# Unpadded weight tiles: a graph attention kernel whose matmuls load 125 columns instead of 128

## What is computed

```python
q = (x @ Wq + bq).reshape(n, H, C)      # k and v likewise, n = 3125, C = 128
alpha = jnp.einsum('ehc,ehc->eh', q[dst], k[src]) / jnp.sqrt(jnp.float32(C))
p = jnp.exp(alpha - amax[dst])          # amax: the largest alpha of each dst
denom = jax.ops.segment_sum(p, dst, num_segments=n) + 1e-16
out = jax.ops.segment_sum(p[:, :, None] * v[src], dst, num_segments=n)
out = out / denom[:, :, None]
out = out.reshape(n, H * C) if concat else out.mean(axis=1)
return out + x @ Ws + bs
...
h = jax.nn.relu(layer1); out = layer2(h); result = layernorm(x + out)
```

## Time and profile before

| | us |
|---|---|
| median of 3 runs | 2020.97 (2019.72 to 2021.14) |
| the profiled execution, its own time | 2020.97 |
| its span in the profile | 2019.2 |
| PE busy | 1820.1 (90%), 14788 matmuls |
| PEld busy | 1356.7 (67%) |
| DVE busy | 1603.9 (79%) |
| ACT busy | 1241.7 (61%) |
| POOL busy | 1162.1 (58%) |

### The profile page before, as it was taken

One profiled execution on the slowest core, in us unless ns is written; L12 is line 12 of the kernel. 1 busy time (PEld: TensorE's weight loads), 2 busy tenths in 40 slices (PEclk: granted clock), 3 DMA queues, 4 the chain that ended last, 5 costly groups with the idle time before them and its releaser, 6 DMA issues. The chain is left out here.

```text
span 2019.2 us, 44528 instructions
## 1 busy us (share of the span) xinstructions
PE 1820.1 (90%) x14788; PEld 1356.7 (67%) x14788; DVE 1603.9 (79%) x4613; ACT 1241.7 (61%) x2055; POOL 1162.1 (58%) x1481
## 2 busy tenths in 40 slices
PE   2876657999999999999999999949889999999998
PEld 1456654777777777777777777736557777777776
DVE  3799986888888888888888888722478888898886
ACT  2665444776777677777777776722156666766666
POOL 3310004776777677767776767611247777767775
PEclk8877778999999999999999999979989999999999
DMA  5059985887788788877877877670169889899996
GB/s 122 1 132 229 229 218 121 155 159 150 150 150 158 146 154 154 154 148 151 157 152 146 154 154 153 119 219 12 30 140 177 171 175 179 168 181 177 169 181 116
DMA packets 771458, 303.31 MB, mean 150 GB/s; under 512 B 657154, under 2 KB 751086, under 8 KB 767979
## 3 DMA queue, kind: packets, MB, share of 16 engines
q1 hardware_dynamic: 767323, 296.42, 73.4%
q10 hardware_dynamic: 3266, 2.36, 0.5%
q0 software_dynamic: 640, 1.63, 0.3%
HBM read 94.57 MB, written 48.45 MB: 71 GB/s over the span
## 5 line engine op out<-in xcount | busy, mean ns | idle before, releaser
L1335 PE MATMUL score_l<-KT,QT_l 128*128 128x512 f16 (+2 forms) x3150 | 772.9, 355 | 13.4 <-DVE piece_max_l L1188 13.0
L1188 DVE CUSTOM_DVE_ANT_0 prob_l<-score_l,mask_l 125x512 f32<-125x512 f32 (+2 forms) x1050 | 642.6, 614 | 166.1 <-PE score_l L1335 162.0
L1037 POOL TENSOR_TENSOR prob_parts_l<-prob_l,prob_parts_l 125x512 f16<-125x512 f32 x600 | 722.2, 1234 | 16.6 <-ACT prob_parts_l L1116 16.6
L1107 ACT ACTIVATE prob_l<-prob_l,neg_max_l 125x1024 f32<-125x1024 f32 (+1 forms) x450 | 524.6, 1166 | 126.6 <-DVE neg_max_l L1196 126.5
L1366 PE MATMUL output_l<-V,prob_flipped_l 128*128 128x256 f16 x2400 | 459.5, 272 | 1.5 <-DMA prob_flipped_l<-prob_parts_l 1.3
L1368 PE MATMUL output_l<-V,prob_flipped_l 128*128 128x128 f16 x2400 | 427.4, 219 | 0.0
L1122 ACT CAST probT_l<-transposed_l 128x375 f16<-128x375 f32 x450 | 209.9, 467 | 335.0 <-PE transposed_l L1360 335.0
L1335 PEld LDWEIGHTS score_l<-KT,QT_l 128*128 128x128 f16 x3150 | 281.4, 99 | 149.9 <-issue 23.9
L1025 POOL CAST QT_l<-q_now_l 128x125 f16<-128x125 f32 x150 | 53.7, 358 | 541.6 <-ACT q_now_l L1094 541.6
L1116 ACT CAST prob_parts_l<-prob_l 125x1024 f16<-125x1024 f32 x300 | 310.0, 1035 | 0.1
L1174 DVE SCALAR_TENSOR_TENSOR mask_l<-mask_l 125x512 f32<-125x512 f32 (+2 forms) x350 | 298.4, 856 | 8.3 <-DMA mask_l<-mask_scratch 8.3
(11 more groups left out here) (168 smaller groups left out, 2006.7 us busy)
## 6 DMA issues: line engine op xcount, KB each, us to landing
mask_scratch<-log SPq DMA_DIRECT2D x79, 448.0 KB
mask_l<-mask_scratch SPq DMA_DIRECT2D x50, 448.0 KB
mask_l<-mask_scratch SPq DMA_DIRECT2D x24, 896.0 KB
mask_l<-mask_scratch SPq DMA_DIRECT2D x24, 471.2 KB
prob_flipped_l<-prob_parts_l SPq DMA_TRANSPOSE x600, 3.3
mask_l<-mask_scratch SPq DMA_DIRECT2D x24, 336.0 KB
hT_scratch<-rowsT_l SPq DMA_DIRECT2D x25, 250.0 KB, 3.5
hT<-hT_scratch SPq DMA_DIRECT2D x6, 1024.0 KB, 13.5
```

What stands on the lines that cost most here:

```text
L1037: pool.tensor_tensor(parts[0:TP, 1, a:b], prob[:, h % 2, a:b], parts[0:TP, 0, a:b], ALU.subtract).then_inc(s_flo, 1)
L1107: act.activation(e, e, ACT.Exp, bias=neg_max[:, h % 2:h % 2 + 1], accum_out=total[:, h % 2, c:c + 1]).then_inc(s_exp, 1)
L1188: dve.tensor_tensor_reduce(out=prob[:, h % 2, a:b], in0=score_bank(h, p)[0:TP, 0:b - a], in1=mask[:, parity, a:b], scale=1.0, scalar=-3.0e ...
L1335: last = pe.matmul(score_bank(h, p)[:, 0:b - a], QT[:, h % 2, i, :], KT[:, h, j, a:b], start=n == 0, stop=n == len(products) - 1)
```

## The change

The padding goes. The weights of scores and products are taken 125 columns wide, the outputs on 125 partitions, and the last block is multiplied with its 53 rows alone. `QT` and `probT` are packed without gaps. Four memsets of DVE and PE's wait for two of them are gone. (The memset of `parts` and those of the `transposed` banks stay.)

```diff
-                link(dve.memset(V[:, NT - 1, :, :, :], 0.0))        # in both projection stages
-        QT = sb("QT", [C, 2, 2, C], F16)
+        QT = sb("QT", [C, 2, 2, TP], F16)
-        probT = sb("probT", [C, NQ, 2, 3, C], F16)
+        probT = sb("probT", [C, NQ, 2, 3 * TP], F16)
-                    pool.tensor_copy(QT[:, u, 0, 0:TP], q_now[:, u, :]).then_inc(s_qh, 1)
+                    pool.tensor_copy(QT[:, u, 0, :], q_now[:, u, :]).then_inc(s_qh, 1)
-                    act.copy(probT[:, q, 0, 0:n, 0:TP], flipped_in_psum(h, q, n)).then_inc(s_hi, 1)
+                    act.copy(probT[:, q, 0, 0:n], flip_bank(h, q)[:, 0:n]).then_inc(s_hi, 1)
-                    dve.tensor_tensor(probT[:, q, 1, 0:n, 0:TP], flipped_in_psum(h, q, n), probT[:, q, 0, 0:n, 0:TP],
+                    dve.tensor_tensor(probT[:, q, 1, 0:n], flip_bank(h, q)[:, 0:n], probT[:, q, 0, 0:n],
-                dve.memset(QT[:, :, :, TP:C], 0.0).then_inc(s_padded, 1)
-                dve.memset(probT[:, :, :, :, TP:C], 0.0).then_inc(s_padded, 1)
-                        last = pe.matmul(score_bank(h, p)[:, 0:b - a], QT[:, h % 2, i, :], KT[:, h, j, a:b],
+                        last = pe.matmul(score_bank(h, p)[0:TP, 0:b - a], QT[:, h % 2, i, :], KT[:, h, j, a:b],
-                    pe.matmul(O[:, 0:2 * C], hi, V[:, b, h, :, :].rearrange("p a c -> p (a c)"),
+                    w = width_of(b)
+                    pe.matmul(O[0:TP, 0:2 * C], hi, V[0:w, b, h, :, :].rearrange("p a c -> p (a c)"),
-                    return pe.matmul(O[:, 0:C], lo, V[:, b, h, 0, :], start=False, stop=stop, skip_group_check=True)
+                    return pe.matmul(O[0:TP, 0:C], lo, V[0:w, b, h, 0, :], start=False, stop=stop, skip_group_check=True)
-                        hi, lo = (probT[:, q, n, i, :] for n in range(2))
+                        hi, lo = (probT[0:width_of(b), q, n, i * TP:(i + 1) * TP] for n in range(2))
-                        hi, lo = (flipped[:, h % 2, n, b, :] for n in range(2))
+                        hi, lo = (flipped[:, h % 2, n, b, 0:TP] for n in range(2))
-                pe.wait_ge(s_padded, 2)
```

More of the change, by code:

```diff
@@ L794, in link @@
                     dve.wait_ge(sem or s_dve, chain[0] if sem is None else 1)
-                link(dve.memset(V[:, NT - 1, :, :, :], 0.0))
                 scales.largest(dve, link, h_max[:, :, :, :])
@@ L888, in attention @@
         s_feat = sem("feat_ready")
-        s_bq, s_clean, s_padded = sem("query_bias_ready"), sem("pads_cleared"), sem("weights_padded")
+        s_bq, s_clean = sem("query_bias_ready"), sem("pads_cleared")
         s_qp, s_qs, s_qh, s_q = (sem(n) for n in ("query_in_psum", "query_scaled", "query_hi_ready", "query_ready"))
@@ L941, in flip_bank @@
             return T[(h * NQ + q) % 2]
-        def flipped_in_psum(h, q, n):
-            return flip_bank(h, q)[:, 0:n * TP].rearrange("k (n i) -> k n i", n=n)
         def half_of(p):
@@ L1024, in query_parts @@
                     pool.wait_ge(s_qs, n + 1).then_inc(s_seen, 1)
-                    pool.tensor_copy(QT[:, u, 0, 0:TP], q_now[:, u, :]).then_inc(s_qh, 1)
+                    pool.tensor_copy(QT[:, u, 0, :], q_now[:, u, :]).then_inc(s_qh, 1)
                     pool.wait_ge(s_qh, n + 1)
-                    pool.tensor_tensor(QT[:, u, 1, 0:TP], q_now[:, u, :], QT[:, u, 0, 0:TP], ALU.subtract).then_inc(s_q, 1)
+                    pool.tensor_tensor(QT[:, u, 1, :], q_now[:, u, :], QT[:, u, 0, :], ALU.subtract).then_inc(s_q, 1)
                 def low_parts(s, h):
@@ L1118, in high_part @@
                 def high_part(s, h, q):
-                    n = len(blocks_in(CUTS[ND + q]))
+                    n = len(blocks_in(CUTS[ND + q])) * TP
                     act.wait_ge(s_tp, NQ * s + q + 1)
                     wait(act, s_pv, NQ * (s - 1) + q + 1)
-                    act.copy(probT[:, q, 0, 0:n, 0:TP], flipped_in_psum(h, q, n)).then_inc(s_hi, 1)
+                    act.copy(probT[:, q, 0, 0:n], flip_bank(h, q)[:, 0:n]).then_inc(s_hi, 1)
                 def tile(t, i, parity):
```

## The result

The changed kernel takes 2048.77 us (median of 4 runs, 2047.49 to 2052.8) against 2020.82: ratio 1.0143, 95% interval 1.0126 to 1.0161. It is 28 us slower; 2033 was forecast, with a range up to 2040. The profiled execution took 2046.03 us, its span is 2043.7.

What follows compares the result with a forecast made beforehand. TensorE was taken to set the pace, with one recurring short stall for DVE's low part. Terms 10.7 + 4.1 - 2.7 + 0 = 12.1 us on the profiled 2020.97 us gave 2033 us, range 2022 to 2040.

Steps and rivals of the forecast that it cites:

- The 53-row products: Last block's 150 matmul pairs with 53 rows instead of 128: same moving columns, so 0 us.
- The sign of being wrong that I had named: At the 53-row pair: a gap of over 100 ns before or behind it would show the prediction wrong.
- switching the row count drains TensorE: Rival: the pipe empties before and after the 53-row pair, 163 ns twice a step, 49 us, so 2082 us; chance 5%.
- The weight load: Loads of 125 columns take 139 ns instead of 98, making 3550 low matmuls 3 ns slower each: 10.7 us.
- The sign that I had named for it: Low matmul L1368 recorded with 222 ns instead of 219, high matmul L1366 unchanged at 272.
- Exposed loads: Where TensorE waits by semaphore, no matmul covers the load: 100 waits at 41 ns, 4.1 us, bounds 2 and 7.
- What the waits give back: Slower loads of some 9 pairs before each wait for DVE's low part only shorten it: 100 x 0.027, -2.7 us.
- the slack swallows half: Rival: DVE's latency loop sets more steps, so slower matmuls replace waiting: +3 to +8 us, say 2026; chance 12%.
- Memsets, casts, starts: Packed casts and subtracts save nothing, dropped memsets lie under other waits, masked scores wait for DMAs: 0, at most -1.1 us.

Runs made afterwards that it cites:

- experiment 1: The changed kernel with the last block multiplied on all 128 rows again and V's two memsets back: 2027.94 us against 2019.98, ratio 1.0038.
- experiment 4: The kernel before, with only the weights of the products (L1366, L1368) taken 125 columns wide, on all 128 rows: 2026.2 us, ratio 1.003.
- experiment 2: The kernel before, padded to 128 columns, with only the last block of values on 53 rows: 2039.21 us, ratio 1.0095.
- experiment 8: The kernel before, with two more matmuls of 256 columns behind the last block's, on 128 rows: 2037.12 us, ratio 1.0083.

## Why the prediction was wrong

- **The 53-row products** are the step that failed. I priced them at 0, by moving columns and by the 53-column transposes. Each change across 64 rows costs 95 ns and an uncovered load: 0.28 us a step in the changed kernel, 42 us, 21 of them seen in the time (experiment 1). The sign of being wrong that I had named, a gap of over 100 ns at the pair, is there: 150 ns from start to start. The transposes were no evidence: they are narrow in columns, not in rows.
- **The rival "switching the row count drains TensorE"** was right in kind and stood at 5%. Its price, 163 ns a change, was taken from latency; measured are 95 ns plus the load, some 140 here. Its total of 2082 left out that waits give back. The Trainium skill ("TensorEngine Tiling (Array Packing)", "Key Properties") says that changing the tiling mode drains the engine, and its "Available Configurations" have modes of 128 and of 64 rows. The traces fit that, with 95 ns at 64 rows and none at 65. That the mode is what changes is argued from this border; no record names it.
- **The weight load** was right in its mechanism and nearly in its size. Loads went from 98 to 138 ns as forecast, and a load beside a low matmul costs 2.4 to 2.5 ns, where I had 3: 8.5 us for 3507 of them against 10.7 for 3550 (experiment 4). The sign that I had named for it did not come: the low matmul keeps 219 ns, and the one behind it is recorded longer and holds longer. Exposed loads of high matmuls cost 33 ns 117 times in experiment 4, 3.9 us against 4.1. Before waits that is 12.4 us; columns and packing cost 8 (experiment 1). With the last block on 128 rows, then, 2028 us would have stood inside the range, though 8 is less than the 12.1 of the sum.
- **What the waits give back** was counted once, 2.7 us, and for the loads alone. The long waits of the table fell by 22. Of 32 us in experiment 2, 13 were hidden, and of 33 in experiment 8, 17. The rival "the slack swallows half", at 12% with +3 to +8 us, is what experiments 4 and 1 measured for the loads (6 and 8). The skip product's wait for ACT, 7 us, was in neither account.
- **Memsets, casts, starts**: 0 forecast. L1196 takes 544 ns against 546, and DVE's masks still wait for their DMA. No experiment took them singly; experiment 1's 8 us would hold any cost of packing too.

## What to carry to other kernels

Don't trim a short last block to its own rows when that takes it to 64 or fewer among matmuls of more: keep it at 65 or more rows, with zeroed operands: 65 rows and 128 took the same time here. Where such blocks can't be avoided, put them side by side, so that the number seldom crosses 64. And when a busy engine is slowed, first look how long it waits in the loop with the others: up to that much of the delay may not be seen.

## What had not been expected of the hardware

- A change between up to 64 and more than 64 weight rows: 95 ns in which nothing starts, then the load in the open, 10 ns for 128 columns of f16 and 50 for 125. 53 and 64 rows cost the same, 65 nothing. Transposes with 53 weight columns of f32 cost nothing (270 ns like their neighbours).
- A load of 125 columns of f16 is recorded with 138 ns instead of 98. Beside 128 moving columns at full clock it costs 2.5 ns, beside 256 or more nothing, behind a wait 33 ns, behind a change of rows 40 ns more than the fast one. The cost stands in the record of the matmul that the load is for, and in the start of the next.
